# Attention of a graph network: every neighbour row by a gather, none read from the table on the chip

## The reference

```
xl, xr = x @ Wl, x @ Wr                              # [3125, 8, 32]
e      = leaky_relu(xl[src] + xr[dst], 0.2)          # [edges, 8, 32]
logits = einsum('ehc,hc->eh', e, att)
m      = segment_max(logits, dst)
p      = exp(logits - m[dst])
out    = segment_sum(p / segment_sum(p, dst)[dst] * xl[src], dst).mean(heads) + bias
```

## Time and profile before

| | us |
|---|---|
| median of 3 executions | 7875.66 |
| lowest, highest | 7863.07, 7904.74 |
| the profiled execution | 7890.42 |
| its span, first to last instruction | 7888.7 |
| mean granted clock of TensorE over the span | 0.827 |
| attention (three layers), from 3324 us of the span on | 4565 |

### The profile page before, as it was taken

How to read it: one execution, slowest core, us unless ns; L and a number is a source line. 1 busy time by engine, 2 the same in 40 slices (tenths; PEclk the granted TensorE clock), 3 DMA queues, 4 the chain that set the end, 5 groups by cost and what they waited for, 6 DMA issues and landing times.

```text
span 7888.7 us, 136475 instructions
## 1 busy us (share of the span) xinstructions
PE 6027.0 (76%) x46669; PEld 3955.1 (50%) x46669; DVE 3734.3 (47%) x7123; ACT 1754.8 (22%) x3748; POOL 3873.9 (49%) x4028
## 2 busy tenths in 40 slices
PE   5888887666666777677788886778878857778787
PEld 4666665566655666534444443344444424444444
DVE  5444443555564555534444445444444544444446
ACT  2222222333330000022222221222222222222221
POOL 4555553444435455355555542555555345555551
PEclk8888886777886777788888887888888879888888
DMA  4444442222212222233333332333333323333332
GB/s 102 129 129 131 128 128 85 53 56 56 57 49 63 62 62 59 57 74 90 88 91 91 91 86 57 84 89 90 88 88 92 87 54 89 88 90 89 93 87 64
DMA packets 689768, 660.52 MB, mean 84 GB/s; under 512 B 398899, under 2 KB 481274, under 8 KB 689082
## 3 DMA queue, kind: packets, MB, share of 16 engines
q1 hardware_dynamic: 555754, 484.41, 20.5%
q0 software_dynamic: 128960, 166.69, 11.1%
q10 hardware_dynamic: 4368, 0.70, 0.1%
HBM read 562.14 MB, written 89.17 MB: 83 GB/s over the span
## 4 chain that ended last, share of the span: by engine, by line
PE 49%; issue 20%; another core or an unknown queue 18%; DVE 7%; ACT 3%; DVEq 2%; DMA 0%; ACTq 0%; POOL 0%; SPq 0%; POOLq 0%
PE ps L1055 14%; PE ps L900 12%; PE ps L994 6%; PE ps L915 2%; PE ps L855 2%; PE ps L1005 2%; PE ps L1015 2%; PE ps L980 1%; PE ps L864 1%; PE ps L974 1%; DVE region L1778 1%; DVE acc L1803 1%; PE ps L842 1%; PE ps L1029 1%
## 5 line engine op out<-in xcount | busy, mean ns | idle before, releaser
L381 POOL DMA_INDIRECT rows<-table,idx x2340 | 2262.4, 967 | 2235.3 <-ACT region L651 1002.6
L1055 PE MATMUL ps<-region,hot 128*128 128x272 f32 x4992 | 1530.4, 458 | 282.6 <-DVE region L1756 149.3
L1055 PEld LDWEIGHTS ps<-region,hot 128*128 128x128 f32 x4992 | 1041.7, 219 | 677.6 <-issue 445.3
L900 PE MATMUL ps<-hot,region 128*128 128x192 bf16 (+1 forms) x8640 | 1120.3, 291 | 322.4 <-issue 291.3
L1803 DVE TENSOR_TENSOR acc<-acc,ps 128x272 f32 x1248 | 545.0, 437 | 1704.9 <-remote 804.5
L662 ACT ACTIVATE region<-ps 128x512 f32<-128x512 f32 x1248 | 677.6, 595 | 2707.6 <-remote 1428.2
L900 PEld LDWEIGHTS ps<-hot,region 128*128 128x128 bf16 x8640 | 911.2, 116 | 467.0 <-issue 391.3
L368 POOL DMA_INDIRECT rows<-table,idx x728 | 700.5, 962 | 530.0 <-PE ps L835 315.8
L994 PE MATMUL ps<-xT,wcat 64*128 64x512 f32 x2496 | 773.6, 697 | 179.3 <-ACT region L662 81.1
L1778 DVE TENSOR_TENSOR region<-ps,region 128x1056 f32<-128x1056 f32 x582 | 725.1, 1252 | 44.5 <-issue 40.9
L398 POOL DMA_INDIRECT rows<-table,idx x480 | 458.7, 956 | 506.6 <-PE ps L927 344.5
(11 more groups left out here) (304 smaller groups left out, 6836.1 us busy)
## 6 DMA issues: line engine op xcount, KB each, us to landing
hot<-hot_dram SPq DMA_DIRECT2D x624, 256.0 KB
turned<-turned_dram SPq DMA_DIRECT2D x624, 128.0 KB
rows<-table,idx POOLq DMA_INDIRECT x3548
hot_dram<-hot SPq DMA_DIRECT2D x104, 512.0 KB
region<-hot_dram SPq DMA_DIRECT2D x90, 512.0 KB
xwin<-table SPq DMA_DIRECT2D x1664, 24.0 KB
region<-d_dram SPq DMA_DIRECT2D x104, 256.0 KB
turned_dram<-turned SPq DMA_DIRECT2D x104, 256.0 KB
```

The source lines that it names most:

```text
L381: pool.indirect_dma_start(rows[:, n % 2, j, :], None, table, bass.IndirectOffsetOnAxis(ap=idx[:, s:s + 1], axis=0)).then_inc(rows_in3[n % ...
L900: mm = pe.matmul(ps[:, GB + i % 2, 224 * j:224 * j + n], bt[b][:, k, at:at + P], tabparts[:, k::FOLD, (2 + s) * C:(3 + s) * C], start=(k = ...
L1055: mm = pe.matmul(ps[:, sum_bank(k, side, i), 0:PC + H], hot[:, b, 4 * side + 2 * i + j, :], px[b][:, 4 * side + 2 * i + j, :], start=(j == ...
```

## The change

All eight slots of every group are gathered. The reading of the eighth row of the odd groups from the chip goes, and all that served it: SP's loads of the source numbers, the one-hot tables, the copy `tabC`, the 12 matmuls, the picking, the masks `spanhot`, their tiles and semaphores, and the waits for them. `rows_in` treats the eighth slot of an odd group as every other. The edge network, which has a reading of its own, and the convolutions stay as they are.

```diff
@@ rows_there
-            return rows_in3[n % 2], 16 * sum(8 - k % 2 for k in range(n % 2, n + 1, 2))
+            return rows_in3[n % 2], 128 * (n // 2 + 1)
@@ pool_attention
-                for j, s in enumerate(piece_slots(g)[0:8 - g % 2]):
+                for j, s in enumerate(piece_slots(g)):
@@ sp_attention
-            def numbers_for(c):
...
-                sp.dma_start(rline1[at % 2].rearrange("p (n e) -> p n e", n=4),
-                             r_dram.rearrange("a (f e) -> (a f) e", f=2)[first:first + 13:4, :].partition_broadcast(P)
-                             ).then_inc(r1_in[at % 2], 16)
-
-            numbers_for(0)
             rows_for(0)
             rows_for(1)
-            numbers_for(1)
             for u in range(G + LAG):
-                if u % 8 == 5:
-                    numbers_for(u // 8 + 2)
@@ act_attention
-                n = 8 - g % 2
-                act.activation(xs[:, (g // 8) % 2, g % 8, 0:n, 0:C], rows[:, (l * G + g) % 2, 0:n, 0:C], ACT.Copy).then_inc(xs_kept, 1)
+                act.activation(xs[:, (g // 8) % 2, g % 8, :, 0:C], rows[:, (l * G + g) % 2, :, 0:C], ACT.Copy).then_inc(xs_kept, 1)
@@ pe_attention, rows_in
-                if g % 2 == 1:
-                    pe.wait_ge(one_kept, (l * G + g) // 2 + 1)
...
-                        elif at < 7 or g % 2 == 0:
+                        else:
                             mm = pe.matmul(ps[q:q + C, XT, j * P:(j + 1) * P],
...
-                        elif s == 0:
-                            pe.matmul(ps[q:q + C, XT, j * P:(j + 1) * P], xs[:, (g // 8) % 2, g % 8, 7, 0:C],
-                                      ident[:, :], start=True, stop=True).then_inc(x_made, 1)
@@ pe_attention, the reading and its waits
-            def read_one(g):
...
-                    if side == 1 and i == 0:
-                        pe.wait_ge(one_picked, (l * G + min(k + LAG + 4, G)) // 2)
...
-            pe.wait_ge(tab_kept, l + 1)
             rows_in(0)
-            read_one(1)
...
-                    pe.wait_ge(one_picked, (l * G + u + 3) // 2)
                     self_sums(u)
-                if u >= 8 and u % 2 == 0 and u + 3 < G:
-                    if k > 0:
-                        pe.wait_ge(att_added, 4 * (l * G + k) - 1)
-                    read_one(u + 3)
...
-                if u < 8 and u % 2 == 0:
-                    pe.wait_ge(zn_read, l * W + min(4 * u + 2, W))
-                    read_one(u + 3)
@@ vector engine
-            def stationary_one(l, c, k):
-            def pick_one(l, g):
...
-                    if k % 2 == 1:
-                        v.wait_ge(one_kept, (l * G + k) // 2 + 1)
...
-                v.tensor_copy(tabC, tabparts[:, :, 2 * C:5 * C]).then_inc(tab_kept, 1)
-                for k in range(FOLD):
-                    stationary_one(l, 0, k)
-                pick_one(l, 1)
```

65 lines of the change are left out of this document (1 added, 64 removed).

## The result

The kernel after took 8136.45 us (median of 4 executions, 8088.26 to 8159.89) beside 7877.76 us of the kernel before: ratio 1.0333, 95% interval 1.0304 to 1.0361, or 259 us longer. Forecast were 134 us and a range up to 8110. The sign held, the size did not: the time lies above the range.

What follows compares the result with a forecast made beforehand. The prediction held that GpSimd's gather bursts bound the attention intervals, not TensorE's work. Its terms, 170 - 41 + 5 = +134 us, gave a median of 8010 us, with an 8-in-10 range of 7850 to 8110.

Steps and rivals of the forecast that it cites:

- The bound: Attention layers: each interval between L655 copies lasts 0.9 us, plus GpSimd's gather burst, plus about 3; TensorE's work is hidden.
- One gather more, +170: Eighth gather in 156 odd groups at L381, 1.25 us a step, half counted where u % 8 = 1: +170 us.
- The reading's tail, -41: Without the reading's matmuls at L1029, the tail behind an even interval's burst shortens, 0.35 us in 117 intervals: -41 us.
- The stop for the picking, 0: L1055's 149.3 us wait for L1756 at the odd interval's start: its removal is worth 0, bound -149.
- the clock after it, 0: L1055 at half clock after the stop, 3.97 instead of 2.02 us: 1.9 us per odd interval might return, counted 0.
- Rival 3: Slower: the gather counts everywhere and longer idling costs TensorE clock in odd intervals; up to +299 us, 8175; chance 0.10.
- Rival 1: The reading made even intervals long, the gather still lengthens odd ones; +19 us, so 7895; chance 0.12.
- Rival 2: TensorE's own work is the pace, the hold only its queue seen late; -312 us, so 7564; chance 0.12.
- Rival 4: The eighth gather finds cover and the stop returns its cost; -41 to +20 us, 7835 to 7896; chance 0.06.
- Odd intervals of 13.5: Sign that the forecast is right: odd intervals between copies take 13.5 us, from 0.9 + 9.75 + 2.9.
- The last even interval of a layer: Sign that the forecast is right: this interval, where gathers have run out, stays nearly unchanged at 8.4 us.
- The last sign: The hold is refuted if the L655 copy comes less than 2 us behind the last gather or moves without it.

Runs made afterwards that it cites:

- the early half: TensorE issues logits and the next group's first product half ahead of the sums' second half; on the kernel after 1.0104, on the kernel before 0.9969.
- SP's alone: Kernel before with SP loading the one-hot halves one step later, so window loads start at the copy; 7709.01 us, ratio 0.9951.
- TensorE's alone: Kernel before with logits and the next group's first product half issued ahead of the sums' second half; 7726.05 us, ratio 0.9969.
- both: Kernel before with TensorE's early first product half and SP's one-hot halves loaded one step later; 7714.79 us, ratio 0.9967.

## Why the prediction came out as it did

- **The bound.** Right in the main. The interval follows the burst, and TensorE's work is not the pace (four gathers on chip B: ratio 0.848; the hold shows on A, B, D, E and F). But the gathers don't hold alone: without SP's window loads the same eight gathers gave 0.989 of before. What the prediction called a hold that the trace doesn't explain is at least in part a slow step, seen in SP's register instructions and in the distance of TensorE's matmuls. "And about 3" behind the burst was right only while the first pair comes out ahead of the burst's end. One reading was off without harm: the chain's 8.20 us from 4037.10 end at 4045.30, in the even interval, and not at the pair of 4057.63.
- **One gather more, +170.** The mechanism was right, the size a little low: 183, 186 and 188 us on three chips, 1.17 to 1.20 per gather. I had counted half a step in the fourth interval (u % 8 = 1); on chip E, with the early half, the odd intervals grew by 1.08 us there and by 0.81 to 1.04 in the other three phases, so the step counts whole.
- **The reading's tail, -41.** Alone 30 us (chip B), with the early half up to 56 (chip E). Right in sign and near in size, but only where the first half of the products gets through; that it is the longer tail, as the prediction said, was not tested.
- **The stop for the picking, 0, and the clock after it, 0.** Here is the step that failed. I wrote of the half-clock batch that follows the stop: "They too end under the hold: 0." That holds for a batch in the odd interval, where half clock was. With the change the half clock went to the batches ahead of the even interval's first half: granted clock at the start of even intervals 0.67 instead of 0.96, of odd ones 0.77 instead of 0.64. The first half is issued at 4.51 us instead of 3.25 in the mean, and in 52 instead of 24 of 123 even intervals its pair at L637 comes out behind the burst, which makes the interval 2.7 us longer. I had looked at what the clock costs TensorE, and not at what stands behind the slowed batch in its queue. The price, measured on chip F: 77 us beside the eighth gather where -30 (chip B) to -56 (chip E) was to be had, so the missing term is 107 to 133 us there. On chip D, where the whole change cost 183 us, it is about 30 if the parts cost there what they did on chip B.
- **Why the phase went over** is settled only in part. The twelve matmuls are not what kept it (chip D: 0.76 against 0.73). The stop itself is left, and no run here put it back alone on a chip with the hold; the wait for an addition was tried alone on chip C only. Nor is it the lost reading alone: on chip B seven gathers without a reading show the clock half way (0.81) and 31 even intervals behind, no more than the 31 of the eighth gather with its reading on the same chip. Only both parts together give 45 to 55. The cause of the shift stays open.
- **Rival 3** (gather counts everywhere, idling costs clock, +299) was nearest: the sign it asked for, a layer's clock falling from 0.86, came (0.845 to 0.847 in the three layers), though not the "under 0.84" named further down. Its gather term, 195, lies about as far from the 183 to 188 measured as the forecast's 170. Its place was wrong: not odd batches that take 1.9 us more, but even first halves. I gave it 0.10 and kept only its lower half in the range; with the whole of it, up to 8175, the range would have held the time.
- **Rival 1** is out: the even intervals did not fall. **Rival 2** is out: with four gathers the same work of TensorE took 1,467 us less, and on chip C, without the hold, the gathers of GpSimd are the pace. **Rival 4** is out.
- **Signs.** Odd intervals of 13.5: right (mean 13.49), with some luck: the forecast added a step of 1.25 us to an interval of 12.3, which is the median before; the mean before was 12.84, and it grew by only 0.65. Even ones of 13.5 to 13.9: wrong (mean 15.11). GpSimd 2,410 us at its gather: 2394.0. The last even interval of a layer "nearly unchanged at 8.4": 9.8, 11.1 and 9.8 us in the three layers, though no gathers run. (Before, it was 10.1, 8.4 and 8.4; the prediction quoted the second.) The one of 11.1 us shows the price of the clock without any hold. L630 at its two ends, which answers to the earlier trace rows:

```profile
L630 ACT ACTIVATE xT<-ps x2: 598/598/599, 6353.0 to 6364.2; 128x512 f32<-128x512 f32 x2
```

And TensorE's timeline in it:

```profile
6352.19 4.00 PE L1008 MATMUL ps<-region,hot 128*128 128x272 f32 x8
...
6356.11 2.54 PE L985 MATMUL ps<-region,attblk 128*32 128x512 f32 x16
...
6358.58 1.13 PE L964 MATMUL ps<-xT,wcat 64*128 64x512 f32 x4
```

The sums take 4.00 us and the logits 2.54, as in the interval of 17.1 us, the first half is issued 5.6 us behind the copy, and the interval is 2.7 us longer than its 8.4 of before. The last sign, a copy that comes less than 2 us behind the last gather or moves without it, was met on chip C: there the copies run in the midst of the gathers, so the hold belongs to some chips and not to the kernel alone.

## What to carry to other kernels

A step that is "under the hold anyway" is free only as long as what stands behind it in the same queue still gets out ahead of the hold's end: ask not only whether the slowed batch has slack, but which instruction comes next and what its result must catch. Where a part is removed, add a term for the parts together: here each part alone was forecast within 15 us of what it measured, and the two together cost some 105 us more than their sum on chips A and F, and some 30 on chip D. And where a result is needed early in another engine's burst, put its work first in the queue: the early first half took 1.5% from the kernel after and 0.3% from the kernel before. The best versions found are the kernel before with either order (SP's alone 0.9951 on chip D, TensorE's alone 0.9969 and both 0.9967 on chip E); on chip C the orders bring nothing.

## What the runs showed of the hardware

- Beside a burst of indirect gathers from GpSimd single register instructions of SP take about 0.7 us, where those of a window load else take 0.03 to 0.07, and matmuls of TensorE's intake are issued 0.7 or 1.4 us apart; 876 of SP's 4,960 in the three layers take over 0.3 us in the kernel after, and none of VectorE's 3,606. One chip of the five in the experiments doesn't show it, and the same kernel takes 5763 us there instead of 7752 to 7873.
- Fewer gathers or fewer loads of SP both shorten the hold: with four gathers the first pair of an even interval stands 1.92 us behind its products, without SP's window loads 0.94, in the kernel after 3.84, and on the chip without the hold 0.07.
- The price of a gather is not far apart on both kinds of chip, for two different reasons: 1.17 to 1.20 us where the burst holds the others; where nothing is held, GpSimd's own 1.25 us a step are the pace, and 156 gathers more came to (5926.6 - 5763.5) / 156 = 1.05 us each. The kernel after itself was not timed on chip C; with an added wait it was 2.7% slower than before there.
- The kernel after cost 3.4% on one chip with the hold and 2.3% on another (1.0339 and 1.0234, intervals apart). What differs between those two was not looked for.
